# Two-layer cross-attention on one core: 32x32 transpositions on VectorE in layer 0, and its exponential as 16 small ScalarE instructions

## The chip, the cores and the metric

The kernel runs on one core of one Trainium2 chip. The metric is device time in microseconds (us) of that core. The kernel before took 2107.89 us in the median of three runs (2104.96 to 2112.77).

## The reference

Two cross-attention layers follow each other on x, 4 batches of 1024 tokens with 1024 features, with one context of 64 rows for each batch. Everything is float32.

```
layer 0   q = x @ Wq + bq            32 heads of 32 features
          k = ctx @ Wk + bk          8 key heads, each shared by 4 query heads
          v = ctx @ Wv + bv
          attn = softmax(q.k / sqrt(32) + mask)      over 64 keys
          x = layernorm(attn.v @ Wo + bo + x) * gamma + beta
layer 1   a = layernorm(ctx); q = x @ Wq.T; k, v = a @ Wk.T, a @ Wv.T
          16 heads of 64, softmax over 64 keys
          x = x + tanh(gate) * (attn.v @ Wo.T)
```

## The kernel before, in words

Every product is made exact enough by splitting both operands in a high and a low part: the high part is a cast to the matmul's float32 format, the low part is what is left. The helper `three` (L53 to L55) then issues three matmuls for one product. Whoever needs a product therefore needs ScalarE for the high part, and VectorE or GpSimd for the low part, of both operands.

The program has three stages: layer 0's attention, layer 0's output (with the preparation of layer 1's matrices in a table of slots), and layer 1. The change lies nearly all in the first stage.

That stage first prepares the context (turned by TensorE, projected to keys and values, split, and stored in scratch memory), and then runs 64 units: 8 blocks of 512 tokens times 8 key heads g, each with its group of 4 query heads. For one unit the steps are:

- the query of 128 features by 512 tokens, 24 matmuls with Wq as weights; ScalarE adds the bias and makes the high part qs (L528), VectorE the low part (L671);
- the scores of 4 x 128 tokens against 4 heads x 64 keys, 12 matmuls with a block-diagonal key tile kb;
- VectorE adds the mask out of PSUM into pr (L677) and takes the maximum of each of 16 (token tile, head) rows (L682); GpSimd subtracts it (L783); ScalarE takes the exponential of all 1024 elements in one instruction (L546); VectorE sums (L694) and inverts (L698); GpSimd multiplies (L786);
- TensorE turns the probabilities, eight transpositions of 128x128 (L411), into PSUM; ScalarE makes the high part pTh (L541), VectorE the low part pTl (L689);
- six matmuls with the block-diagonal value tile vb; ScalarE copies the result to ot (L533), and SP stores it in o_scratch.

The tiles of x are turned by TensorE as well, eight transpositions (L328) for each tile of 128 tokens; `next_x(u)` says in which units: every second one, for the block that follows. ScalarE and VectorE split them (L490, L610).

The order is written out by hand for each engine in a loop over u, and a wait on a semaphore stands ahead of each instruction that needs one. In its iteration u an engine works on the query of unit u, the scores of unit u-1 and the probabilities of unit u-2, and so on: the units overlap. An engine takes its instructions strictly in this order. SP loads kb and vb for each unit out of scratch memory, four DMAs each, and issues them in its own order. Mask and x tiles are double-buffered, pr is held three times, the turned probabilities once.

Of the kernel before, what the change touches and what calls it, by code (L numbers as in the profile page):

```python
# [16 lines left out]
F32 = mybir.dt.float32  # L17
# [6 lines left out]
P = 128  # L24
# [51 lines left out]
def layer0(nc, ps, ident, d, w):  # L76
    with ExitStack() as mem:
# [13 lines left out]
        xr = [at(f"xr{i}", 144 + 4 * i, [P, D]) for i in range(2)]  # L91
# [9 lines left out]
        vst = [at(f"vst{r}", 140 + 2 * r, [P, 2, KV0], F32R) for r in range(2)]  # L101
        kf, vf = at("kf", 196, [P, 2, CTX]), at("vf", 198, [P, 2, KV0])

        qs = [[at(f"qs{i}{x}", 152 + 4 * i + 2 * j, [P, BLK], F32R) for j, x in enumerate("hl")] for i in range(2)]
        kb = [at(f"kb{i}", 160 + 2 * i, [P, 2, GRP, KEYS], F32R) for i in range(2)]
        vb = [at(f"vb{i}", 164 + 2 * i, [P, 2, 2, P], F32R) for i in range(2)]
        pr = [at(f"pr{i}", 168 + 4 * i, [P, TPB, GRP, KEYS]) for i in range(3)]
        pT = [at(f"pT{x}", 180 + 4 * j, [P, 2, BLK], F32R) for j, x in enumerate("hl")]
        ot = [at(f"ot{i}", 188 + 2 * i, [P, BLK]) for i in range(2)]
# [25 lines left out]
        bq, bk, bv_row = part(0, KT), part(8, 2), at("bv", 200, [P, KV0])  # L135
# [8 lines left out]
        S, TR = ps[:, 1024:2048], ps[:, 2048:3072]  # L144
        V = [ps[:, 3072 + HALF * i:][:, :HALF] for i in range(2)]
        C2 = ps[:, 0:2048]
        O, TT = Q, S
# [11 lines left out]
        wq_ld, x_ld, k_ld, v_ld, o_st = sems("wq_ld", KT), sems("x_ld", 2), sems("k_ld", 2), sems("v_ld", 2), sems("o_st", 2)  # L159
# [16 lines left out]
        def sync_attention(sp):  # L176
            sp.dma_start(ctx[:], d["ctx"].rearrange("(r p) d -> p r d", p=P)).then_inc(ctx_ld, 16)
            for n in range(2):
                sp.dma_start(xr[n][:], d["x"][P * n:P * (n + 1), :]).then_inc(x_ld[n], 16)
# [7 lines left out]
            for k in range(3):  # L187
                sp.dma_start(wqr[:, k], w["Wq0"][P * k:P * (k + 1), :]).then_inc(wq_ld[k], 16)
            for n in range(2, 4):
                sp.wait_ge(x_turned, n - 1)  # L190
                sp.dma_start(xr[n % 2][:], d["x"][P * n:P * (n + 1), :]).then_inc(x_ld[n % 2], 16)
            for k in range(3, KT):
                sp.dma_start(wqr[:, k], w["Wq0"][P * k:P * (k + 1), :]).then_inc(wq_ld[k], 16)
            sp.dma_start(mask[0][:], d["mask"][0:BLK, :].rearrange("(m p) s -> p m s", p=P)).then_inc(mask_ld, 16)
            for h in range(2):
                sp.wait_ge(k_hi, h + 1)
                sp.wait_ge(k_lo, h + 1)
                sp.dma_start(d["k"][h], f32(kst[h][:]).rearrange("p b x s -> p b (x s)")).then_inc(kv_st, 16)
            for r in range(2):
                sp.wait_ge(v_hi, r + 1)  # L200
                sp.wait_ge(v_lo, r + 1)
                sp.dma_start(d["v"][r], f32(vst[r][:])).then_inc(kv_st, 16)
            sp.wait_ge(kv_st, 64)
            sp.wait_ge(zeroed, 4)

            def load_k(u):
                t, g = divmod(u, KT)
                h, a = divmod(g, 4)
                src = d["k"][h, HD0 * a:HD0 * (a + 1), t // 2, :].rearrange("p (x s) -> p x s", x=2)
                for j in range(GRP):  # L210
                    sp.dma_start(f32(kb[u % 2][HD0 * j:HD0 * (j + 1), :, j, :]), src).then_inc(k_ld[u % 2], 16)

            def load_v(u):
                t, g = divmod(u, KT)
                r, a = divmod(t // 2, 2)
                src = d["v"][r, KEYS * a:KEYS * (a + 1), :, HD0 * g:HD0 * (g + 1)]
                for i in range(2):
                    for c in range(2):
                        o = HD0 * (2 * c + i)
                        sp.dma_start(f32(vb[u % 2][KEYS * i:KEYS * (i + 1), :, c, o:o + HD0]), src).then_inc(v_ld[u % 2], 16)  # L220

            load_k(0)
            load_v(0)
            for u in range(UNITS + 3):
                t, g = divmod(u, KT)
                if u < UNITS and u % 2 == 0 and (n := 4 + u // 2) < NTILE:
                    after(sp, x_turned, n - 1)
                    sp.dma_start(xr[n % 2][:], d["x"][P * n:P * (n + 1), :]).then_inc(x_ld[n % 2], 16)
                if u + 1 < UNITS:
                    after(sp, scores, u)  # L230
                    load_k(u + 1)
                if g == 2 and t + 1 < NBLK:
                    after(sp, s_read, 8 * t)
                    sp.dma_start(mask[(t + 1) % 2][:], d["mask"][BLK * (t + 1):BLK * (t + 2), :]
                                 .rearrange("(m p) s -> p m s", p=P)).then_inc(mask_ld, 16)
                if 2 <= u <= UNITS:
                    after(sp, pv, u - 2)
                    load_v(u - 1)
                if u >= 3:
                    v = u - 3  # L240
# [8 lines left out]
        def sync_output(sp):  # L249
            def load_chunk(c):  # L250
                t, a = divmod(c, BLK // CHUNK)
                for i in range(2):
                    sp.wait_ge(o_st[i], 16 * 4 * (t + 1))
                after(sp, o_done, 4 * (c - 1))
                sp.dma_start(oc[c % 2][:], d["o"][t, :, :, CHUNK * a:CHUNK * (a + 1)].rearrange("g p c -> p g c"))\
                    .then_inc(oc_ld[c % 2], 16)
# [68 lines left out]
        def tensor_attention(pe):  # L325
            def turn(out, src, done):
                for k in range(KT):
                    last = nc.tensor.transpose(out[:, P * k:P * (k + 1)], src[:, P * k:P * (k + 1)], ident[:])  # L328
                last.then_inc(done, 1)

# [6 lines left out]
            def turn_x(n):  # L337
                pe.wait_ge(x_ld[n % 2], 16 * (n // 2 + 1))
# [885 lines left out]
```

## Time and profile before

| | |
|---|---|
| median of 3 runs | 2107.89 us |
| the profiled execution | 2110.65 us, its span 2108.9 us |
| mean granted TensorE clock | 0.976 |
| TensorE busy (matmul) | 1960.3 us, 93% |
| VectorE busy | 1003.8 us, 48% |
| GpSimd busy | 763.4 us, 36% |
| ScalarE busy | 580.7 us, 28% |

The shares are means over three stages with different limits, so they say little on one of them. The views in the section on rows are taken from the stage that is changed. In a timeline a row is one instruction or several alike: its start, its duration, engine, line, operation, output and inputs, and in brackets the engine's idle time before it with what ended it. In a table of windows a row gives a stretch, its length, the busy time of PE, PEld, DVE, ACT and POOL with the number of instructions, PEclk, the DMA engines' share and GB/s. Matmuls overlap, so their pace is the distance from start to start, and not the duration. PEclk is the clock that TensorE was granted, where 1.00 is 2.4 GHz and 0.50 is 1.2 GHz.

### The profile page before, as it was taken

How to read it: one execution, taken by the hardware profiler on the slowest of the kernel's cores; microseconds unless marked ns; L12 is line 12 of the kernel's file. 1: busy time of each engine (PE TensorE's matmuls, PEld its weight loads, DVE VectorE, ACT ScalarE, POOL GpSimd, SP SyncE). 2: the span in 40 equal slices, each digit the busy share in tenths (PEclk: the TensorE clock that was granted, in tenths of full speed). 3: DMA queues.
4: the chain of work that ended last, by engine and by line, in shares of the span. 5: the costliest groups of instructions: out<-in, count | busy, mean ns of one | idle time of the engine just before them, and what ended most of it. 6: DMA issues, size and time to landing. Idle time of an engine off the chain costs nothing. (4 is left out here: it accounts for less than half of the span.)

```text
span 2108.9 us, 24271 instructions
## 1 busy us (share of the span) xinstructions
PE 1960.3 (93%) x9664; PEld 1613.5 (77%) x9664; DVE 1003.8 (48%) x1061; ACT 580.7 (28%) x674; POOL 763.4 (36%) x480
## 2 busy tenths in 40 slices
PE   6999999999999869999999995899999999999998
PEld 5777777777777657788888874688778878877887
DVE  6555555555555544444444433623453264345322
ACT  4333333333333333222323221311221131122110
POOL 1333333333333344546455453511341152134111
PEclk8999999999999979999999997999999999999999
DMA  6212212222223146565546643331331133113100
GB/s 238 59 55 60 69 58 69 60 68 61 68 60 118 40 164 202 197 219 180 198 167 211 203 160 137 136 116 41 119 121 50 50 121 120 40 40 130 50 30 30
DMA packets 181694, 227.77 MB, mean 108 GB/s; under 512 B 70480, under 2 KB 130000, under 8 KB 181584
## 3 DMA queue, kind: packets, MB, share of 16 engines
q1 hardware_dynamic: 181584, 226.20, 31.6%
q8 instruction: 81, 1.33, 0.3%
q14 instruction: 29, 0.24, 0.0%
HBM read 141.20 MB, written 84.93 MB: 107 GB/s over the span
## 5 line engine op out<-in xcount | busy, mean ns | idle before, releaser
L1159 POOL TENSOR_TENSOR prob<-prob,mx 128x1024 f32<-128x1024 f32 x32 | 61.0, 1907 | 452.2 <-DVE mx L1126 452.2
L53 PE MATMUL ps<-Ah,x2Tl 128*128 128x512 f32 x512 | 205.2, 401 | 8.2 <-POOL Al L939 7.2
L783 POOL TENSOR_TENSOR pr<-pr,small 128x1024 f32<-128x1024 f32 x64 | 121.9, 1905 | 246.1 <-DVE small L682 246.1
L53 PE MATMUL ps<-Bh,probTl 128*128 128x512 f32 x512 | 202.3, 395 | 2.4 <-DVE probTl L1141 2.4
L55 PE MATMUL ps<-Ah,x2Th 128*128 128x512 f32 x512 | 201.9, 394 | 0.0
L54 PE MATMUL ps<-Al,x2Th 128*128 128x512 f32 x512 | 201.8, 394 | 0.0
L55 PE MATMUL ps<-Bh,probTh 128*128 128x512 f32 x512 | 199.7, 390 | 0.0
L54 PE MATMUL ps<-Bl,probTh 128*128 128x512 f32 x512 | 199.2, 389 | 0.0
L786 POOL TENSOR_TENSOR pr<-pr,small 128x1024 f32<-128x1024 f32 x64 | 122.1, 1907 | 212.6 <-DVE small L698 212.6
L1122 DVE SCALAR_TENSOR_TENSOR prob<-ps,bias 128x1024 f32<-128x1024 f32 x32 | 39.1, 1223 | 238.0 <-PE ps L55 238.0
L677 DVE TENSOR_TENSOR pr<-ps,mask 128x1024 f32<-128x1024 f32 x64 | 78.4, 1224 | 147.9 <-PE ps L55 147.9
L541 ACT CAST pTh<-ps 128x1024 fp32r<-128x1024 f32 x64 | 65.2, 1018 | 271.6 <-PE ps L411 271.6
L798 POOL TENSOR_TENSOR xb<-xb,bo 128x1024 f32<-128x1024 f32 x32 | 78.6, 2458 | 157.6 <-DMA xb<-in_x_dram 149.3
L689 DVE TENSOR_TENSOR pTl<-ps,pTh 128x1024 fp32r<-128x1024 f32 x64 | 78.4, 1225 | 117.9 <-ACT pTh L541 117.9
L738 DVE TENSOR_TENSOR y<-ps,xb 128x512 f32<-128x512 f32 x64 | 44.2, 690 | 178.2 <-PE ps L55 171.2
L53 PEld LDWEIGHTS ps<-Ah,x2Tl 128*128 128x128 f32 x512 | 98.3, 192 | 28.4 <-issue 9.0
L53 PE MATMUL ps<-wo0h,oc0l 128*128 128x512 f32 x256 | 102.7, 401 | 15.8 <-POOL oc0l L793 15.8
L55 PEld LDWEIGHTS ps<-Ah,x2Th 128*128 128x128 f32 x512 | 97.6, 191 | 20.8
L1057 ACT CAST x2Th<-ps 128x1024 fp32r<-128x1024 f32 x32 | 32.5, 1015 | 292.4 <-PE ps L1001 292.4
L54 PEld LDWEIGHTS ps<-Al,x2Th 128*128 128x128 f32 x512 | 98.0, 191 | 19.5
L53 PEld LDWEIGHTS ps<-Bh,probTl 128*128 128x128 f32 x512 | 96.2, 188 | 21.4 <-DVE probTl L1141 2.6
L55 PEld LDWEIGHTS ps<-Bh,probTh 128*128 128x128 f32 x512 | 96.1, 188 | 20.4
(186 smaller groups left out, 4900.3 us busy)
## 6 DMA issues: line engine op xcount, KB each, us to landing
xr<-in_x_dram SPq DMA_DIRECT2D x32, 512.0 KB, 3.7
o_scratch<-ot SPq DMA_DIRECT2D x64, 256.0 KB, 2.3
xb<-in_x_dram SPq DMA_DIRECT2D x32, 512.0 KB, 5.1
ocr<-o_scratch SPq DMA_DIRECT2D x16, 1024.0 KB, 6.5
a_scratch<-ost SPq DMA_DIRECT2D x64, 256.0 KB, 3.0
x_scratch<-y SPq DMA_DIRECT2D x32, 512.0 KB, 3.3
b_scratch<-ost SPq DMA_DIRECT2D x64, 256.0 KB, 2.3
x2t<-x_scratch SPq DMA_DIRECT2D x32, 512.0 KB, 3.3
```

The lines of the kernel that those rows point to most:

```text
L53: nc.tensor.matmul(out, a[1], b[0], start=start, stop=False)
L54: nc.tensor.matmul(out, a[0], b[1], start=False, stop=False)
L55: return nc.tensor.matmul(out, a[0], b[0], start=False, stop=stop)
L541: nc.scalar.copy(pT[0][:].rearrange("p c n -> p (c n)"), TR).then_inc(p_hi, 1)
L677: nc.vector.tensor_tensor(p[:], S.rearrange("p (m j s) -> p m j s", m=TPB, j=GRP), mask[t % 2][:].unsqueeze(2).to_broadcast([P, TPB, GRP, ...
L689: nc.vector.tensor_tensor(pT[1][:].rearrange("p c n -> p (c n)"), TR, f32(pT[0][:]).rearrange("p c n -> p (c n)"), ALU.subtract).then_inc( ...
L738: nc.vector.tensor_tensor(y[n % 3][:, cols], O[half], xb[n % 2][:, cols], ALU.add).then_inc(y_done, 1)
L783: nc.gpsimd.tensor_tensor(heads, heads, mx.unsqueeze(2).to_broadcast([P, TPB * GRP, KEYS]), ALU.subtract)\
L786: nc.gpsimd.tensor_tensor(heads, heads, rs.unsqueeze(2).to_broadcast([P, TPB * GRP, KEYS]), ALU.mult)\
L798: nc.gpsimd.tensor_tensor(xb[n % 2][:], xb[n % 2][:], bo0[:], ALU.add).then_inc(xbo, 1)
L1122: nc.vector.scalar_tensor_tensor(out=pr[:], in0=S.rearrange("p (h s) -> p h s", h=H1), scalar=SCALE1, in1=bias[:, bass.ds(b, 1), :].to_bro ...
L1159: nc.gpsimd.tensor_tensor(pr[:], pr[:], mx[:].unsqueeze(2).to_broadcast([P, H1, KEYS]), ALU.subtract).then_inc(centered, 1)
```

## The change

TensorE no longer turns x or the probabilities. VectorE's transposition turns 32x32 blocks only, so the rest of the way is taken by other orders of the data:

- x, Wq, the mask, the context and the stored output are loaded and stored with other access patterns. An x tile now comes in as four DMAs of 32 partitions each, and VectorE turns it in one instruction into xTr (`turn_x`). Wq's rows, keys and values are permuted to match, and keys and values are stored together in one scratch tensor in 12 DMAs.
- The token order inside a block is (token // 4, token % 4), so the query is read out of PSUM with a step of 4, and ot is written with a step of 4. The loads of o_scratch in the output stage are eight DMAs of 32 partitions in place of one.
- The probabilities are turned by one VectorE transposition of 128x1024 elements (L695 of the changed kernel) into pTr, in SBUF. ScalarE copies the high part from there, and the low part goes from VectorE to GpSimd.
- VectorE takes the maximum negated. GpSimd no longer subtracts it, and VectorE no longer sums: ScalarE takes the exponential in 16 instructions of 64 elements with the negated maximum as bias, and each writes its sum to sm.
- The scores have two PSUM regions, since the one for the turned data is free. pr is held twice in place of three times, the turned probabilities twice in place of once.
- The values of a unit are now multiplied three iterations behind the query in place of two, and the loop is one iteration longer.
- In the output stage GpSimd no longer waits for the last stores of ot ahead of its clearing of bd.

The core of the diff:

```
@@ tensor_attention, loop over u
-                    after(pe, s_read, v)
+                    after(pe, s_read, v - 1)
 ...
-                n = next_x(u) if u < UNITS else None
-                if n is not None:
-                    after(pe, p_lo, u - 2)
-                    turn_x(n)
 ...
-                    pe.wait_ge(probs, v + 1)
 ...
-                    for c in range(2):
-                        for m in range(TPB):
-                            last = nc.tensor.transpose(TR[:, BLK * c + P * m:][:, :P], pr[v % 3][:, m, 2 * c:2 * c + 2, :]
-                                                       .rearrange("p j s -> p (j s)"), ident[:])
-                    last.then_inc(p_turned, 1)
 ...
-                if u >= 2:
-                    v = u - 2
+                if u >= 3:
+                    v = u - 3
                     pe.wait_ge(p_lo, v + 1)

@@ scalar_attention
+            for u in range(UNITS + 4):
+                if u >= 4:
+                    v = u - 4
                     act.wait_ge(pv, v + 1)
                     after(act, o_st[v % 2], 16 * (v // 2))
+                    nc.scalar.copy(ot[v % 2][:].rearrange("p (j i m) -> p j m i", j=GRP, m=TPB),
+                                   V[v % 2].rearrange("p (j m i) -> p j m i", j=GRP, m=TPB)).then_inc(o_ev, 1)
+                if 2 <= u < UNITS + 2:
+                    v = u - 2
+                    act.wait_ge(maxed, v + 1)
+                    after(act, recips, v)
+                    heads = pr[v % 2][:].rearrange("p j m s -> p (j m) s")
+                    for e in range(TPB * GRP):
+                        last = nc.scalar.activation(heads[:, e], heads[:, e], ACT.Exp, bias=mx[:, e:e + 1],
+                                                    accum_out=sm[:, e:e + 1])
+                    last.then_inc(exped, 1)
+                if u < UNITS:
+                    if (n := next_x(u)) is not None:
+                        split_x(n)
+                    act.wait_ge(q_done, u + 1)
+                    after(act, scores, u - 1)
+                    nc.scalar.activation(qs[u % 2][0][:], Q[u % 2].rearrange("p (n m) -> p m n", m=TPB), ACT.Identity,
+                                         bias=bq[:, u % KT:u % KT + 1]).then_inc(q_hi, 1)
                 if 2 <= u < UNITS + 2:
                     v = u - 2
                     act.wait_ge(p_turned, v + 1)
+                    nc.scalar.copy(pT[v % 2][0][:], pTr[v % 2][:]).then_inc(p_hi, 1)

@@ vector_attention
+            for u in range(UNITS + 2):
+                if 1 <= u <= UNITS and (n := next_x(u - 1)) is not None:
+                    split_x(n)
+                if u >= 2:
+                    v = u - 2
+                    dve.wait_ge(exped, v + 1)
+                    after(dve, probs, v)
+                    nc.vector.reciprocal(rs, sm).then_inc(recips, 1)
+                if u < UNITS and (n := next_x(u)) is not None:
+                    turn_x(n)
+                if 1 <= u <= UNITS:
 ... mask addition, then
+                    nc.vector.tensor_reduce(mx, p[:].rearrange("p j m s -> p (j m) s"), AX_X, ALU.max, negate=True).then_inc(maxed, 1)
                 if u >= 2:
                     v = u - 2
+                    dve.wait_ge(probs, v + 1)
+                    after(dve, pv, v - 1)
+                    nc.vector.transpose(pTr[v % 2][:].rearrange("p b j n -> p b (j n)").rearrange("p b (h i) -> p h b i", i=32),
+                                        pr[v % 2][:].rearrange("p j m (b i) -> p (j m) b i", b=2)).then_inc(p_turned, 1)
+                if u < UNITS:
+                    dve.wait_ge(q_hi, u + 1)
 ... the low part of the query

@@ pool_attention
+            for u in range(2, UNITS + 3):
+                if u >= 3:
+                    v = u - 3
+                    pool.wait_ge(p_hi, v + 1)
+                    nc.gpsimd.tensor_tensor(pT[v % 2][1][:], pTr[v % 2][:], f32(pT[v % 2][0][:]), ALU.subtract).then_inc(p_lo, 1)
+                if 2 <= u < UNITS + 2:
+                    v = u - 2
+                    pool.wait_ge(recips, v + 1)
+                    nc.gpsimd.tensor_tensor(heads(v), heads(v), rs.unsqueeze(2).to_broadcast([P, TPB * GRP, KEYS]), ALU.mult)\
+                        .then_inc(probs, 1)

@@ sync_output, load_chunk
+                for i in range(2):
+                    for j in range(GRP):
+                        sp.dma_start(oc[c % 2][32 * j:32 * (j + 1), :, P * i:P * (i + 1)],
+                                     d["o"][t, :, 32 * (2 * a + i):32 * (2 * a + i + 1), P * j:P * (j + 1)]
+                                     .rearrange("g p c -> p g c")).then_inc(oc_ld[c % 2], 16)
```

The order of instructions shows what the loops come to. ScalarE before, in an iteration that splits a tile of x, in the middle of the stage (the semaphores that an instruction waits for stand in brackets; a_centered comes from GpSimd, a_p_turned and a_pv from TensorE):

```order
L528 ACTIVATE qs0h<-ps,small 128x512 [waits a_scores,a_q_done]
L533 COPY ot_90<-ps 128x512 [waits a_o_st0,a_pv]
L490 CAST xT1h<-ps 128x8x128 [waits a_x_turned]
L541 CAST pTh<-ps 128x1024 [waits a_pv,a_p_turned]
L546 ACTIVATE pr_85<-pr_85 128x1024 [waits a_centered]
```

ScalarE in the changed kernel, one iteration of the same kind (a_maxed, a_p_turned and a_x_turned come from VectorE now):

```order
L514 COPY ot_96<-ps 128x4x4x32 [waits a_o_st1,a_pv]
L522 ACTIVATE pr_88,small<-pr_88,small 128x64 [waits a_recips,a_maxed]
L522 ACTIVATE pr_88,small<-pr_88,small 128x64 x15
L476 CAST xT1h<-xT1r 128x8x128 [waits a_x_turned]
L530 ACTIVATE qs1h<-ps,small 128x512 [waits a_scores,a_q_done]
L535 CAST pT1h<-pT1r 128x1024 [waits a_p_turned]
```

The exponentials now stand directly behind the copy to ot, ahead of the high parts of x, of the query and of the probabilities. The cast to pT, which waits for VectorE, stands last.

VectorE before, one iteration with the split of an x tile:

```order
L671 SCALAR_TENSOR_TENSOR qs0l<-ps,small,qs0h 128x512 [waits a_q_hi]
L677 TENSOR_TENSOR pr_85<-ps,mask_92 128x1024 [waits a_scores,a_p_turned]
L682 TENSOR_REDUCE small<-pr_85 128x16 [waits a_centered,a_s_read]
L610 TENSOR_TENSOR xT1l<-ps,xT1h 128x8x128 [waits a_x_hi]
L689 TENSOR_TENSOR pTl<-ps,pTh 128x1024 [waits a_p_hi]
L694 TENSOR_REDUCE small<-pr_85 128x16 [waits a_exped]
L698 RECIPROCAL small<-small 128x16 [waits a_probs,a_summed]
```

VectorE in the changed kernel, an iteration that turns an x tile (L600):

```order
L674 RECIPROCAL small<-small 128x16 [waits a_probs,a_exped]
L600 STREAM_TRANSPOSE xT1r<-xr_59 128x4x8x32 [waits a_q_done,a_x_ld1]
L684 TENSOR_TENSOR pr_87<-ps,mask_97 128x4x4x64 [waits a_scores]
L690 TENSOR_REDUCE small<-pr_87 128x16 [waits a_exped,a_s_read]
L695 STREAM_TRANSPOSE pT1r<-pr_88 128x16x2x32 [waits a_pv,a_probs]
L699 SCALAR_TENSOR_TENSOR qs1l<-ps,small,qs1h 128x512 [waits a_q_hi]
```

The reciprocal has moved ahead of the mask addition (L684) and waits for ScalarE there (a_exped); the low part of the query stands last.

## Rows read from the trace of the kernel before

**Rows 1.** Table of windows, the stretch of layer 0's attention.

```profile
57.10:725.50 668.40, 622.82 (x3356) 511.77 (x3355) 388.01 (x406) 231.43 (x278) 240.19 (x126) 1.00 0.23 66
```

**Rows 2.** Query for line L677: count, durations, first and last start.

```profile
L677 DVE TENSOR_TENSOR pr<-ps,mask x64: 1223/1225/1226, 57.1 to 725.5; 128x1024 f32<-128x1024 f32 x64
```

**Rows 3.** Timeline of TensorE in one step: start, duration, what, idle time before.

```profile
399.99 0.40 PE L54 MATMUL ps<-xT0l,wq0h 128*128 128x512 f32 x1
400.23 0.40 PE L55 MATMUL ps<-xT0h,wq0h 128*128 128x512 f32 x1
...
402.94 1.06 PE L411 MATMUL ps<-ident,pr 128*128 128x128 f32 x8 [0.93 <-DVE xT1l L610]
...
409.35 0.28 PE L54 MATMUL ps<-kb,qs1h 128*128 128x256 f32 x1
409.46 0.28 PE L55 MATMUL ps<-kb,qs1h 128*128 128x256 f32 x1
```

**Rows 4.** Timeline of VectorE, the same step.

```profile
399.18 1.23 DVE L677 TENSOR_TENSOR pr<-ps,mask 128x1024 f32<-128x1024 f32 x1 [2.12 <-PE ps L55]
400.44 1.22 DVE L682 TENSOR_REDUCE small<-pr 128x16 f32<-128x1024 f32 x1
401.58 1.22 DVE L610 TENSOR_TENSOR xT1l<-ps,xT1h 128x1024 fp32r<-128x1024 f32 x1
...
407.48 0.25 DVE L698 RECIPROCAL small<-small 128x16 f32<-128x16 f32 x1
407.65 0.66 DVE L671 SCALAR_TENSOR_TENSOR qs1l<-ps,small,qs1h 128x512 fp32r<-128x512 f32 x1
410.94 1.23 DVE L677 TENSOR_TENSOR pr<-ps,mask 128x1024 f32<-128x1024 f32 x1 [2.63 <-PE ps L55]
```

**Rows 5.** Timeline of ScalarE, the same step.

```profile
404.05 1.02 ACT L541 CAST pTh<-ps 128x1024 fp32r<-128x1024 f32 x1 [3.07 <-PE ps L411]
404.95 1.06 ACT L546 ACTIVATE pr<-pr 128x1024 f32<-128x1024 f32 x1
```

**Rows 6.** Groups of ScalarE by shape: count, busy us, mean ns, idle before.

```profile
L546 ACT ACTIVATE pr<-pr 128x1024 f32<-128x1024 f32 x64 | 67.9, 1060 | 26.4 <-POOL pr L783 26.4
...
L533 ACT COPY ot<-ps 128x512 f32<-128x512 f32 x64 | 37.7, 589 | 65.1 <-PE ps L55 65.0
...
L528 ACT ACTIVATE qs1h<-ps,small 128x512 fp32r<-128x512 f32 x32 | 22.0, 687 | 2.8
...
L553 ACT CAST oc0h<-ocr 128x1024 fp32r<-128x1024 f32 x16 | 16.0, 1049 | 8.8 <-DMA ocr<-o_scratch 8.7
...
L1060 ACT ACTIVATE gt<-gate 128x1 f32<-128x1 f32 x1 | 0.2, 202 | 12.9 <-DMA gate<-in_L_xattn_gate_dram 12.9
```

**Rows 7.** Timeline of GpSimd, the same step.

```profile
407.81 1.91 POOL L786 TENSOR_TENSOR pr<-pr,small 128x1024 f32<-128x1024 f32 x1 [4.16 <-DVE small L698]
```

**Rows 8.** Groups of GpSimd by shape.

```profile
L786 POOL TENSOR_TENSOR pr<-pr,small 128x1024 f32<-128x1024 f32 x64 | 122.1, 1907 | 212.6 <-DVE small L698 212.6
...
L793 POOL TENSOR_TENSOR oc0l<-ocr,oc0h 128x1024 fp32r<-128x1024 f32 x16 | 39.0, 2458 | 21.4 <-ACT oc0h L553 21.4
```

**Rows 9.** Table of windows in layer 1, around an idle TensorE.

```profile
1508.00:1512.00 4.00, 3.05 (x12) 2.77 (x13) 3.29 (x3) 0.98 (x1) 4.00 (x2) 0.58 0.00 0
1512.00:1516.00 4.00, 4.00 (x19) 3.28 (x18) 1.22 (x1) 0.04 (x1) 2.58 (x2) 1.00 0.57 184
```

**Rows 10.** Timeline of TensorE there, at the idle time.

```profile
1508.95 1.97 PE L1045 MATMUL ps<-ident,prob 128*128 128x128 f32 x8 [2.31 <-POOL prob L1165]
```

**Rows 11.** Timeline of ScalarE, the last copy to ot.

```profile
741.91 0.59 ACT L533 COPY ot<-ps 128x512 f32<-128x512 f32 x1 [4.28 <-PE ps L55]
```

**Rows 12.** Query for line L255, the loads of chunks.

```profile
L255 SPq DMA_DIRECT2D ocr<-o_scratch x16: 377/381/527, 743.9 to 1245.9; - x16
...
  ACT oc1h L553: 10.0, 4
  ACT oc0h L553: 8.7, 4
```

More of the change, by code:

```diff
@@ L186, in sync_attention @@
             sp.dma_start(bet1[:], row(w["beta1"], D)).then_inc(gb_ld, 16)
-            for k in range(3):
-                sp.dma_start(wqr[:, k], w["Wq0"][P * k:P * (k + 1), :]).then_inc(wq_ld[k], 16)
+            load_wq(0)
             for n in range(2, 4):
                 sp.wait_ge(x_turned, n - 1)
[L191 to L194, printed above, removed]
+                load_x(n)
+            for k in range(2, KT, 2):
+                load_wq(k)
+            load_mask(0)
             for h in range(2):
@@ L197, in sync_attention @@
                 sp.wait_ge(k_lo, h + 1)
-                sp.dma_start(d["k"][h], f32(kst[h][:]).rearrange("p b x s -> p b (x s)")).then_inc(kv_st, 16)
+                for a in range(4):
+                    sp.dma_start(d["kv"][h, :, :, a, :P].rearrange("b p c -> p b c"),
+                                 f32(kst[h][32 * a:32 * (a + 1)]).rearrange("p b x s -> p b (x s)")).then_inc(kv_st, 16)
             for r in range(2):
@@ L201, in sync_attention @@
                 sp.wait_ge(v_lo, r + 1)
-                sp.dma_start(d["v"][r], f32(vst[r][:])).then_inc(kv_st, 16)
-            sp.wait_ge(kv_st, 64)
+                for h in range(2):
+                    sp.dma_start(d["kv"][h, :, :, :, P + 64 * r:P + 64 * (r + 1)].rearrange("b p g c -> (b p) g c"),
+                                 f32(vst[r][:, 4 * h:4 * (h + 1)]).rearrange("p g x d -> p g (x d)")).then_inc(kv_st, 16)
+            sp.wait_ge(kv_st, 16 * 12)
             sp.wait_ge(zeroed, 4)
@@ L227, in sync_attention @@
                     after(sp, x_turned, n - 1)
-                    sp.dma_start(xr[n % 2][:], d["x"][P * n:P * (n + 1), :]).then_inc(x_ld[n % 2], 16)
-                if u + 1 < UNITS:
-                    after(sp, scores, u)
+                    load_x(n)
+                if 1 <= u and u + 1 < UNITS:
+                    sp.wait_ge(scores, u)
                     load_k(u + 1)
+                if 3 <= u <= UNITS:
+                    sp.wait_ge(pv, u - 2)
+                    load_v(u - 1)
                 if g == 2 and t + 1 < NBLK:
                     after(sp, s_read, 8 * t)
[L234 to L240, printed above, removed]
+                    load_mask(t + 1)
+                if u >= 4:
+                    v = u - 4
                     sp.wait_ge(o_ev, v + 1)
@@ L325, in tensor_attention @@
         def tensor_attention(pe):
[L326 to L329, printed above, removed]
             def turn_ctx():
@@ L385, in tensor_attention @@
                 if u < UNITS:
-                    query(range(0, 2))
+                    query(range(0, 4))
                 if 1 <= u <= UNITS:
@@ L421, in tensor_attention @@
                     for c in range(2):
-                        last = three(nc, V[v % 2], [vb[v % 2][:, x, c] for x in (0, 1)], [pT[x][:, c] for x in (0, 1)],
+                        last = three(nc, V[v % 2], [vb[v % 2][:, c, x] for x in (0, 1)], [pT[v % 2][x][:, c].rearrange("p j n -> p (j n)") for x in (0, 1)],
                                      c == 0, c == 1)
@@ L563, in diagonal @@
                     r = slice(HD1 * h, HD1 * (h + 1))
[L564 removed]
+                    last = nc.scalar.copy(bd[i][0][r, :, h, :].rearrange("p b (r i) -> p b r i", r=2), PJ[i][r].rearrange("p (r b i) -> p b r i", r=2, b=BATCH))
                 last.then_inc(bd_hi, 1)
@@ L815, in pool_output @@
             pool.wait_ge(pv, UNITS)
-            for i in range(2):
-                pool.wait_ge(o_st[i], 16 * UNITS // 2)
             for i in range(2):
```

211 lines of the change are left out of this document (86 added, 125 removed).

## The prediction

> **What bounds the kernel now.** I read the stretch of layer 0's attention first, since nearly all edits lie in its 64 steps. The table of windows shows TensorE busy 622.82 of 668.40 us there, at a granted clock of 1.00, beside 388.01 us on VectorE, 231.43 us on ScalarE and 240.19 us on GpSimd [rows 1]. The query for the mask addition L677 gives the step: 64 of them from 57.1 to 725.5 us, so 668.4 / 63 = 10.61 us each [rows 2]. The timelines by engine then show one step at close range. TensorE runs one matmul of 512 columns each 0.24 us or a little less and one of 256 columns each 0.12 us, and spends 1.06 us on the eight turns of probabilities, with 0.93 us of idle time ahead of them [rows 3]. VectorE waits 2.12 and 2.63 us for TensorE before L677 [rows 4], and ScalarE 3.07 us for the turned probabilities [rows 5]. So TensorE sets the step, and the others have room.
>
> **The change on TensorE.** Per step it loses eight turns of probabilities, and in 28 of the 63 steps eight turns of x. What stays is 30 matmuls of 512 columns (24 for the query, 6 for the values) and 12 of 256: 30 x 0.23 + 12 x 0.12 = 8.3 us [rows 3]. If TensorE still set the step, 63 x (10.61 - 8.3) = 146 us would go. Whether it does depends on the loop that the new order builds between ScalarE and VectorE.
>
> **The new loop.** On VectorE the reciprocal of head group u-2 now stands ahead of the mask addition of u-1 and waits for the sixteenth exponential of u-2. The transposition of u-2 stands behind mask addition and maximum of u-1. On ScalarE the copy of the turned probabilities of u-2 waits for that transposition, and the exponentials of u-1 stand behind this copy and behind the copy to ot. So the chain is closed: exponentials of u-2, reciprocal, mask addition of u-1, maximum of u-1, transposition of u-2, copy to pTh, copy to ot, exponentials of u-1. Before, none of it was serial in this way: the exponential of u-1 shared no chain with the reciprocal of the group before. Its terms, from start to start:
> - copy to ot: 0.589 us [rows 6] less the 0.1 us by which ScalarE instructions in a row overlap (404.05 + 1.02 against the next start at 404.95, [rows 5]): 0.49. It is now written with a step of four elements, which no row shows; nothing to a second 0.59, and I take nothing.
> - reciprocal: 407.48 to 407.65, 0.17, and 0.1 for a semaphore (it ends at 407.73 and GpSimd starts at 407.81, [rows 4, 7]): 0.27.
> - mask addition: 399.18 to 400.44 [rows 4]: 1.26. Same elements, other order of writing; I take the same.
> - maximum, now negated: 400.44 to 401.58 [rows 4]: 1.14.
> - transposition of 1024 elements in 32x32 blocks: no row shows one. Every VectorE pass over 1024 f32 elements in rows 4 takes 1.21 to 1.23 us; I take 1.2 and a semaphore of 0.05: 1.25. Bounds: 0.6 (two elements at a time) to 2.4 (two passes).
> - copy to pTh, now out of SBUF: 1.049 us as for oc0h [rows 6], less 0.1: 0.95.
> Together 0.49 + 0.27 + 1.26 + 1.14 + 1.25 + 0.95 = 5.36 us beside the exponentials. The GpSimd product of 1.907 us [rows 8] runs beside mask addition and maximum (2.4 us) and costs nothing; without that cover it would add 1.9. The removed centring, the removed sum and the lo part that goes from VectorE to GpSimd (1.2 us off VectorE, 2.458 us as for oc0l onto GpSimd, [rows 8]) are not in the loop: GpSimd then holds 1.9 + 2.5 = 4.4 us per step. In the 28 steps that turn x, the transposition of x stands between reciprocal and mask addition: 28/63 x 1.15 = 0.51 us on the mean. The loop is 5.87 us plus E, the time of sixteen exponentials.
>
> **E.** One exponential of 1024 takes 1060 ns and a one-element activation 202 ns [rows 6], so (1060 - 202) / 1023 = 0.84 ns per element, and 64 elements take 255 ns. The bias from memory adds 687 - 589 = 98 ns (qs1h against ot, both 128x512, [rows 6]): about 350 ns for one alone, 0.24 us from start to start at the usual overlap of 0.11. What the sum taken along costs no row shows. Lower bound nothing: 0.24 each, E = 3.8. Upper bound a separate instruction of 202 ns with no overlap at all: 0.55 each, E = 8.8. With the read overlapped it is 0.24 + 0.09 = 0.33, with a read that waits for its exponential's end 0.35 + 0.20 - 0.11 = 0.44. I take 0.36, nearer to the overlapped form because the rows in rows 5 overlap: E = 5.8, against one exponential of 1.06 us before. Loop: 5.87 + 5.8 = 11.65 us.
>
> By the Trainium skill, ScalarE: Activation LUTs, section What ACT_TABLE_LOAD costs, an activation with a bias from memory takes 280 ns + 0.833 ns per element and overlaps its neighbour by about 93 ns, which is 240 ns for 64 elements; the trace's rows agree with that. It has no price for the accumulator output, so by it alone E is an estimated 3.84 us. The skill's VectorE: DVE Perf Modes, section on the TRN2 errata, speaks against the change: each small tile pays the fixed latency again, and it wants 512 elements or more. The rows here carry the same point: 16 x 0.24 = 3.8 us against 1.06 us.
>
> **Steps and edges.** 63 x (11.65 - 10.61) = +66 us. TensorE then idles about 3.3 us a step, in one piece ahead of the scores, where it waits for qs lo, which stands last in VectorE's iteration. Such a gap has a price in this trace: after 2.31 us of idle time the granted clock was 0.58 over the 4 us in which TensorE resumed [rows 9, 10]. Here that costs some 1.5 us of TensorE per step, and lies inside the gap: 8.3 + 1.5 is under 11.65, so I count 0. Start: VectorE transposes four x tiles more, 4 x 1.15 = 4.6, and two units more of stores and loads stand ahead of the loop: +6. End: one stage more of pipeline behind the last mask addition, where before it took 741.91 + 0.59 - 725.5 = 17.0 us [rows 2, 11]: the maximum, E, reciprocal, product, transposition, copy, lo part, values, copy to ot make about 21: +4. Output stage: each of 16 chunk loads is eight DMAs in place of one at 0.38 us of issue, 2.7 us later, with smaller packets, and ScalarE waited for these loads eight times [rows 12]; 0 to 8 x 2.7 = 22, I take +3, as TensorE hides most waits there. SP gets three more x DMAs in every second step (4 x 0.38 us by the same row), which lie in its waits. Sum: 66 + 6 + 4 + 3 = +79 on the profiled run's own 2110.65 us (its span of 2108.9 and 1.75 around it), 2190 us; that run lies 2.8 us above the median of 2107.89, so I say 2186 (2189.4 less 2.8). The edges are 13 us of it.
>
> **Rivals.**
> - The sum costs nothing (pitch 0.24). The loop is 9.7 us, 63 x -0.9 + 13 = -44: 2064 us. For it: the overlap seen between ScalarE instructions, and that TensorE's floor of 8.3 leaves room. Against it: an output of its own to write sixteen times. The deciding point is E = 10.4 - 5.87 = 4.5 us, a pitch of 0.28. Faster than before below it.
> - The sum is read serially, 0.44 to 0.55 each: E 7.0 to 8.8, loop 12.9 to 14.7, and with the 13 us of the edges +157 to +271: 2265 to 2379 us. A transposition at two passes gives the same size at my pitch: (1.15 + 0.51) x 63 = +105 on the forecast, 2291 us. For it: the added bounds all lie above. Against: no such gap in the rows.
> - TensorE's clock stays at its lower level of 1.2 GHz because of the gaps: its 8.3 us become 16.6, it sets the step, and 63 x 6.0 + 13 gives 2499 us. Against it: the clock was back at 1.00 in the 4 us after the fall [rows 9].
> - Nothing measurable (the pitch happens on 0.28): 2108.
>
> **Numbers.** Forecast 0.57, its own range 2130 to 2265 (pitch 0.30 to 0.44); sum free 0.19; serial read or slow transposition 0.18; clock 0.02; no change 0.04. Half a per cent is about what a measurement of this kernel tells from no change. Faster 0.19, same 0.04, slower 0.77. The range 2085 to 2300 leaves out about 0.12 of the free case and 0.08 of the dear ones.
>
> **What would show it.** In the new profile: 64 mask additions about 11.6 us apart; VectorE's reciprocal waiting for ScalarE's exponentials; ScalarE waiting some 4 us for the transposition each step; TensorE waiting for qs lo ahead of the scores and busy about 75% of the stretch. The start-to-start time of the small exponentials decides: at 0.24 the kernel is faster, at 0.36 or more it is slower. A mask addition that waits for TensorE again, or ScalarE idle while VectorE waits for scores, would make the loop wrong.

## The result and the profile after

The changed kernel takes 2203.96 us (median of 4 runs, 2200.70 to 2204.68), the kernel before 2108.78 us (4 runs, 2104.96 to 2112.77). The ratio is 1.0448, 95% interval 1.0426 to 1.0471: 4.5% slower. The forecast was 2186 us, range 2085 to 2300. The profiled span is 2202.3 us at a mean granted clock of 0.943, 93.4 us longer than before.

The attention of layer 0 first. The query for the mask addition, now L684, and the table of windows over its stretch answer to [rows 1, 2]:

```profile
L684 DVE TENSOR_TENSOR pr<-ps,mask x64: 1160/1184/1225, 65.6 to 795.5; 128x1024 f32<-128x1024 f32 x64
```

```profile
65.60:795.50 729.90, 575.03 (x2628) 472.58 (x2626) 335.48 (x370) 519.10 (x2229) 279.52 (x124) 0.91 0.20 60
```

729.9 / 63 = 11.59 us a step where it was 10.61. TensorE's share fell from 93% to 79% of the stretch, and ScalarE's busy time more than doubled, from 231.43 to 519.10 us. The timeline of VectorE shows one turn of the loop (columns as in [rows 4]):

```profile
401.31 0.25 DVE L674 RECIPROCAL small<-small 128x16 f32<-128x16 f32 x1 [5.54 <-ACT pr L522]
401.48 1.16 DVE L684 TENSOR_TENSOR pr<-ps,mask 128x1024 f32<-128x1024 f32 x1
402.67 1.22 DVE L690 TENSOR_REDUCE small<-pr 128x16 f32<-128x1024 f32 x1
403.81 1.24 DVE L695 STREAM_TRANSPOSE pT0r<-pr 128x1024 f32<-128x1024 f32 x1
404.97 0.71 DVE L699 SCALAR_TENSOR_TENSOR qs0l<-ps,small,qs0h 128x512 fp32r<-128x512 f32 x1
412.33 0.25 DVE L674 RECIPROCAL small<-small 128x16 f32<-128x16 f32 x1 [6.66 <-ACT pr L522]
412.50 1.19 DVE L600 STREAM_TRANSPOSE xT0r<-xr 128x1024 f32<-128x1024 f32 x1
```

And that of ScalarE in the same step:

```profile
405.08 1.05 ACT L535 CAST pT0h<-pT0r 128x1024 fp32r<-128x1024 f32 x1 [3.23 <-DVE pT0r L695]
406.03 1.08 ACT L514 COPY ot<-ps 128x512 f32<-128x512 f32 x1
406.90 0.33 ACT L522 ACTIVATE pr<-pr,small 128x64 f32<-128x64 f32 x1
407.13 0.19 ACT L522 ACTIVATION_READ_ACCUMULATOR pr<-pr,small 128x1 f32 x1
407.23 0.33 ACT L522 ACTIVATE pr<-pr,small 128x64 f32<-128x64 f32 x1
...
412.12 0.19 ACT L522 ACTIVATION_READ_ACCUMULATOR pr<-pr,small 128x1 f32 x1
413.72 1.04 ACT L476 CAST xT0h<-xT0r 128x1024 fp32r<-128x1024 f32 x1 [1.42 <-DVE xT0r L600]
```

Each of the two engines stands while the other works: VectorE 5.54 and 6.66 us for the sixteenth exponential, ScalarE 3.23 us for the turned probabilities. The mask addition waits for nothing in this step (7.6 us in 8 of the 64), where before it waited 2.12 and 2.63 us for TensorE [rows 4]. TensorE now waits for VectorE, here 0.99 us for the low part of the query (PE timeline), and over the stretch 101 us for this and 52.5 us for the last turned x tile at seven block starts:

```profile
405.73 0.39 PE L53 MATMUL ps<-kb,qs0l 128*128 128x256 f32 x1 [0.99 <-DVE qs0l L699]
```

The groups of ScalarE by shape in this stretch, which answer to [rows 6]:

```profile
L522 ACT ACTIVATE pr<-pr,small 128x64 f32<-128x64 f32 x1008 | 334.6, 337 | 0.0
L522 ACT ACTIVATION_READ_ACCUMULATOR pr<-pr,small 128x1 f32 x1008 | 193.0, 191 | 0.0
L514 ACT COPY ot<-ps 128x512 f32<-128x512 f32 x61 | 66.5, 1090 | 0.0
```

Each exponential with a sum is two instructions, 337 and 191 ns, and a pair starts 0.33 us after the last one (406.90, 407.23).

By stages, the 93.4 us of the span are the differences between first and last starts in the two traces:

| stretch | before | after | measured | predicted |
|---|---|---|---|---|
| start to the first mask addition | 57.1 | 65.6 | +8.5 | +6 |
| 63 steps | 668.4 | 729.9 | +61.5 | +66 |
| last mask addition to the first y | 44.7 | 51.5 | +6.8 | +4 |
| first to last y (output stage) | 521.6 | 536.2 | +14.6 | +3 |
| last y to the end | 817.1 | 819.1 | +2.0 | 0 |

The output stage is the one far off. Its loads and who waited for them (us in all, times), from the query for L274, which answers to [rows 12]:

```profile
L274 SPq DMA_DIRECT2D ocr<-o_scratch x128: 303/451/1857, 818.8 to 1338.3; - x128
...
  ACT oc0h L542: 16.1, 5
  ACT oc1h L542: 11.9, 4
```

Theory after this reading: the loop between ScalarE and VectorE sets the step; the change holds a gain (the turns taken off TensorE) and a loss (the sixteen exponentials), tied by the order of the loop; and the output stage loses by the eight loads of each chunk. Rival: the loss lies in the transpositions or in TensorE's lower clock, and the exponentials are incidental.

### The profile page after: what moved, and what is told of

It is laid out like the page before. It is cut to its first block and busy times, and to the rows that moved or that the text cites. A ratio compares the mean times of both kernels' runs of the same rounds, so it can differ in the third digit from the quotient of the medians.

```text
span 2202.3 us, 24852 instructions
## 1 busy us (share of the span) xinstructions
PE 1911.2 (87%) x8896; PEld 1572.3 (71%) x8896; DVE 958.1 (44%) x1029; ACT 874.9 (40%) x2658; POOL 806.0 (37%) x480
## 3 DMA queue, kind: packets, MB, share of 16 engines
q1 hardware_dynamic: 205184, 226.21, 31.9%
q8 instruction: 74, 1.21, 0.2%
## 5 line engine op out<-in xcount | busy, mean ns | idle before, releaser
L522 ACT ACTIVATE pr<-pr,small 128x64 f32<-128x64 f32 x1024 | 339.9, 337 | 0.0
L793 POOL TENSOR_TENSOR pr<-pr,small 128x1024 f32<-128x1024 f32 x64 | 122.0, 1906 | 280.9 <-DVE small L674 280.9
L522 ACT ACTIVATION_READ_ACCUMULATOR pr<-pr,small 128x1 f32 x1024 | 196.0, 191 | 0.0
L674 DVE RECIPROCAL small<-small 128x16 f32<-128x16 f32 x64 | 16.2, 253 | 392.6 <-ACT pr L522 392.6
L805 POOL TENSOR_TENSOR xb<-xb,bo 128x1024 f32<-128x1024 f32 x32 | 77.4, 2419 | 183.3 <-DMA xb<-in_x_dram 174.9
L53 PE MATMUL ps<-xT0h,wq0l 128*128 128x512 f32 x256 | 107.3, 419 | 37.8 <-DVE xT0l L607 37.8
L53 PE MATMUL ps<-xT1h,wq0l 128*128 128x512 f32 x256 | 107.6, 420 | 30.0 <-DVE xT1l L607 30.0
L789 POOL TENSOR_TENSOR pT1l<-pT1r,pT1h 128x1024 fp32r<-128x1024 f32 x32 | 89.2, 2788 | 115.4 <-ACT pT1h L535 115.4
L1086 ACT CAST probTh<-ps 128x1024 fp32r<-128x1024 f32 x32 | 32.5, 1016 | 211.8 <-PE ps L1050 211.8
```

The costliest lines, as they stand in the source:

```text
L53: nc.tensor.matmul(out, a[1], b[0], start=start, stop=False)
L522: last = nc.scalar.activation(heads[:, e], heads[:, e], ACT.Exp, bias=mx[:, e:e + 1], accum_out=sm[:, e:e + 1])
L789: nc.gpsimd.tensor_tensor(pT[v % 2][1][:], pTr[v % 2][:], f32(pT[v % 2][0][:]), ALU.subtract).then_inc(p_lo, 1)
L793: nc.gpsimd.tensor_tensor(heads(v), heads(v), rs.unsqueeze(2).to_broadcast([P, TPB * GRP, KEYS]), ALU.mult)\
L805: nc.gpsimd.tensor_tensor(xb[n % 2][:], xb[n % 2][:], bo0[:], ALU.add).then_inc(xbo, 1)
```

## Experiments

All ratios are to the kernel before on the same chip, where its median was 2108.2 to 2109.4 us. "Step" is the mean distance of two mask additions. A block is eight steps, those of one group of 512 tokens. The edits are shortened to what they change, some of them in words.

| kernel | us | ratio, 95% | step, us |
|---|---|---|---|
| before | 2108.78 | 1 | 10.61 |
| changed | 2203.96 | 1.0426 to 1.0471 | 11.59 |
| no_sum | 2118.47 | 1.0027 to 1.0062 | 10.27 |
| turn_only | 2027.55 | 0.9599 to 0.9631 | 8.87 |
| exp_only | 2334.78 | 1.1050 to 1.1088 | 14.18 |
| ot_plain | 2186.99 | 1.0354 to 1.0389 | 11.29 |
| chunk_one | 2184.64 | 1.0337 to 1.0377 | 11.59 |
| late_cast | 2083.28 | 0.9854 to 0.9925 | 9.75 |
| turn_early | 2000.45 | 0.9464 to 0.9511 | 8.43 |
| turn_late_early | 1984.22 | 0.9390 to 0.9437 | 8.19 |
| exps_late_early | 2041.52 | 0.9662 to 0.9705 | 9.03 |
| store_four | 1968.28 | 0.9313 to 0.9352 | 8.20 |

**no_sum**: the changed kernel without the sum output; sm is filled once, so the probabilities are not divided by their sum.

```
- nc.scalar.activation(..., ACT.Exp, bias=mx[:, e:e + 1], accum_out=sm[:, e:e + 1])
+ nc.scalar.activation(..., ACT.Exp, bias=mx[:, e:e + 1])
```

> The changed kernel, whose sixteen exponentials don't take the sum along; sm is filled once with 64, so the probabilities come out unnormalised by their true sum. Loop theory (ScalarE and VectorE form one serial chain, and the exponentials' pace is a term of it): the pair of exponential and read takes 0.333 us from start to start, the exponential alone should take 0.24, so the chain loses 16 x 0.093 = 1.5 us a step; steps of 10.1 us, kernel 2204 - 63 x 1.5 = 2110 us. Rival (TensorE with its gaps, or ScalarE's busy time, sets the step): ScalarE's busy time falls too, but a step set by TensorE would not move, 2204 us.

Confirmed in the main: 2118 us where 2110 was expected. ScalarE's timeline:

```profile
400.07 1.10 ACT L514 COPY ot<-ps 128x512 f32<-128x512 f32 x1
400.95 1.29 ACT L522 ACTIVATE pr<-pr,small 128x64 f32<-128x64 f32 x5
```

Sixteen exponentials then take 3.92 us, 0.245 each. The sum output costs 0.09 us each, and 2203.96 - 2118.47 = 85 us in all, nearly the whole loss. Inside a block the step falls by 1.49 us (11.07 to 9.58, and 12.14 to 10.66 with a turn of x), the 1.5 that was expected; the mask addition's waits for TensorE at block starts grow from 7.6 to 18.4 us and take the rest back. This is the forecast's rival "sum free", and it came out near the time of before, not below; the section on the prediction says why.

**turn_only**: the changed kernel with maximum, centring, one exponential and sum as before. **exp_only**: the kernel before with the sixteen exponentials alone:

```
(in words)
- pool: centre pr by mx;  act: exp of 1024;  dve: sum of pr
+ dve: maximum negated;   act: 16 exp of 64 with bias=mx, accum_out=sm
```

> The changed kernel with all its transpositions on VectorE, but the softmax as before: GpSimd subtracts the maximum, one exponential of 1024, VectorE sums. Loop theory: the chain exponential, sum, reciprocal, mask addition, maximum, transposition, cast, copy to ot is 0.96 + 0.05 + 1.14 + 0.17 + 1.19 + 1.14 + 1.27 + 0.95 + 0.87 = 7.7 us, 8.9 in the steps that turn x, below or at TensorE's 8.3 and its waits: steps of 8.4 to 8.9 us, kernel 2204 - 63 x 2.9 = 2020 us, range 2000 to 2040, which is faster than the 2109 of before. Rival (the transpositions themselves cost the time, by VectorE's load or strided operands): 2110 us or more.

> The kernel before with only the softmax edit: sixteen exponentials with the maximum as bias and the sum taken along, TensorE still turns x and the probabilities. Loop theory: VectorE's reciprocal of unit v stands ahead of the low part of the next query there, so the chain is exponentials 5.4, reciprocal 0.3, low part 0.7, scores 1.5, mask addition 1.25, maximum 1.2, 10.3 us and semaphores of 0.3, 10.6, against 10.61 of before, and 1 us more in the steps in which TensorE turns x: steps of 10.6 to 11.2 us, 2110 to 2150 us. Rival (the small exponentials cost by ScalarE's load alone, which has room): 2109 us, no change. Rival (the exponentials are the whole loss, whatever stands around them): 2204 us.

turn_only confirmed its expectation: the transpositions on VectorE alone gain 81 us. exp_only missed it by 185 us: alone, the exponentials cost 226 us, not 1 to 41. The two effects do not add (-81 + 226 is not +95). ScalarE and then VectorE in exp_only:

```profile
407.40 0.33 ACT L548 ACTIVATE pr<-pr,small 128x64 f32<-128x64 f32 x1
407.64 0.19 ACT L548 ACTIVATION_READ_ACCUMULATOR pr<-pr,small 128x1 f32 x1
407.73 0.67 ACT L528 ACTIVATE qs1h<-ps,small 128x512 fp32r<-128x512 f32 x1
408.30 0.57 ACT L533 COPY ot<-ps 128x512 f32<-128x512 f32 x1
415.48 1.01 ACT L541 CAST pTh<-ps 128x1024 fp32r<-128x1024 f32 x1 [6.62 <-PE ps L411]
```

```profile
408.43 0.75 DVE L675 SCALAR_TENSOR_TENSOR qs1l<-ps,small,qs1h 128x512 fp32r<-128x512 f32 x1 [0.32 <-ACT qs1h L528]
411.32 1.22 DVE L681 TENSOR_TENSOR pr<-ps,mask 128x1024 f32<-128x1024 f32 x1 [2.15 <-PE ps L55]
```

In that order the query's high part is queued behind the exponentials (402.41 to 407.83). Its low part, the scores, nine query matmuls and the turns of the probabilities follow in turn, and only then the cast and the next exponentials (at 416.39, so this turn of the loop is 13.98 us). TensorE stands on the loop there:

```profile
409.23 0.39 PE L53 MATMUL ps<-kb,qs1l 128*128 128x256 f32 x1 [2.35 <-DVE qs1l L675]
...
411.44 0.63 PE L54 MATMUL ps<-xT1l,wq0h 128*128 128x512 f32 x1
411.87 0.63 PE L55 MATMUL ps<-xT1h,wq0h 128*128 128x512 f32 x1
...
414.41 0.27 PE L411 MATMUL ps<-ident,pr 128*128 128x128 f32 x1
```

Its matmuls of 512 columns are 0.43 us apart here, against 0.24 in [rows 3]. The table of windows gives the granted clock, 1.00 where TensorE resumes after 2.35 us of idle time and 0.50, the lower of its two levels (1.2 GHz), behind it:

```profile
408.00:410.00 2.00, 0.77 (x6) 0.77 (x7) 0.86 (x2) 0.86 (x2) 1.81 (x1) 1.00 0.00 0
411.00:413.00 2.00, 2.00 (x7) 1.61 (x6) 1.64 (x2) 0.00 (x0) 0.00 (x0) 0.50 0.08 16
```

For the same matmuls TensorE is busy 709.4 us over the steps where it was 622.8 before, so the clock accounts for at most 87 of the 226 us, an upper bound, and the serial order for the larger part. I had left both, the place of the query's part and the clock, out of the expectation. In the changed kernel TensorE is off the loop, and the same sixteen instructions cost less there: 176 us, from turn_only's 2027.55 to 2203.96.

**ot_plain**: ot is copied in the order of PSUM, with no step, so the tokens are in a wrong order in the output.

```
- nc.scalar.copy(ot[...] "p (j i m) -> p j m i", V[...] "p (j m i) -> p j m i")
+ nc.scalar.copy(ot[v % 2][:], V[v % 2])
```

> The changed kernel, whose copy to ot is written in plain order and no longer with a step of four, so the tokens come out in another order. Loop theory: the copy is a term of the chain and falls from 1.09 to 0.59 us as in the kernel before, so 0.4 to 0.5 us a step go: 2204 - 63 x 0.45 = 2176 us. Rival (the copy lies beside the chain): 2204 us.

Partly: the copy falls from 1090 to 580 ns, the step by 0.30 us and the time by 17 us, where 0.45 a step was expected. Inside a block the step falls by 0.38 us (11.07 to 10.68, 12.14 to 11.77), which is what the copy loses from start to start (0.87 to 0.48): it is a full term of the loop. Most of the rest is taken back at block starts, where the mask addition's waits for TensorE grow from 7.6 to 12.0 us. The edit changes only the order in which SBUF is written, PSUM is read in the same order in both, so the writing is what costs. The step of four in it was taken at nothing in the prediction.

**chunk_one**: the changed kernel with one DMA for each chunk instead of eight, in the order of before, so o's tokens and heads reach the wrong places.

> The changed kernel with one DMA for each chunk of o_scratch as before, so the output stage reads its tokens and features in another order. Issue theory (eight issues keep SP from its other transfers and delay the chunk): the output stage gives back most of its 14.6 us and the first chunk comes 4 us sooner, 2204 - 15 = 2189 us, range 2185 to 2195. Rival (the output stage is longer for another reason): 2204 us.

Confirmed, 0.4 us below the range: the attention is unchanged, and first to last y is 519.0 us against 536.2 (521.6 before). The first y comes 1.9 us sooner, not 4. ScalarE's groups again wait about as in [rows 6, 12], 9.5 and 10.0 us, and the time falls by 19.3 us. GpSimd's wait for the loads of xb, which SP issues behind the eight, was 149.3 us before and 174.9 in the changed kernel, and is 154.3 here.

```profile
L539 ACT CAST oc0h<-ocr 128x1024 fp32r<-128x1024 f32 x16 | 16.0, 1048 | 9.5 <-DMA ocr<-o_scratch 9.5
```

**late_cast**: the copy to pTh, the lo part and the values one iteration later, with three turned buffers. The loop then has neither cast nor transposition in it.

```
- if 2 <= u < UNITS + 2:  v = u - 2;  copy(pT[v % 2][0], pTr[v % 2])
+ if 3 <= u < UNITS + 3:  v = u - 3;  copy(pT[v % 3][0], pTr[v % 3])
```

> The changed kernel, sixteen exponentials and all, with one move: ScalarE casts the turned probabilities of a unit one iteration later, behind the next unit's exponentials, and the steps behind it (lo part, values, copy to ot) follow one iteration later; the turned probabilities are held three times. Loop theory: transposition, cast and copy to ot drop out of the chain, which leaves exponentials 5.4, semaphore 0.1, reciprocal 0.17, mask addition 1.19, maximum 1.14 and a semaphore, 8.1 us (9.2 in steps that turn x), beside ScalarE's own 5.3 + 0.95 + 0.87 + 0.58 = 7.7 us and TensorE's 8.3: steps of 8.6 us plus some 0.5 for the waits at the starts of blocks, 2204 - 63 x 2.5 + 4 = 2050 us. Rival (the exponentials' own 4 us more of ScalarE are the loss wherever they stand): 2204 us.

The loop was the bound: 1.84 us a step and 121 us less, by an edit that removes no work, and this version is 1.1% faster than before. The size was over-expected: 2083 us, not 2050. The exponentials now wait for the maximum only 1.5 us in the whole stretch, so the loop through VectorE is open. VectorE still waits for the last exponential in each step (2.66 and 3.70 us), as ScalarE's own queue is the longest now: it is busy 515.6 of 614.0 us and waits 40 us more for turned x tiles. From mask addition to mask addition a step inside a block is 9.06 or 9.19 us, where 8.6 was expected. The mean of 9.75 comes from the block starts, where TensorE waits up to 5.4 us for the low part of the last x tile and the next mask addition for TensorE; they cost about 45 us (this stretch less that of exps_late_early below, which has the same steps inside a block), where 0.5 us a step, 32 us, was expected:

```profile
400.99 0.26 DVE L675 RECIPROCAL small<-small 128x16 f32<-128x16 f32 x1 [3.70 <-ACT pr L523]
...
406.42 2.08 DVE L608 TENSOR_TENSOR xT1l<-xT1r,xT1h 128x1024 fp32r<-128x1024 f32 x1
411.16 0.25 DVE L675 RECIPROCAL small<-small 128x16 f32<-128x16 f32 x1 [2.66 <-ACT pr L523]
...
438.77 1.19 DVE L685 TENSOR_TENSOR pr<-ps,mask 128x1024 f32<-128x1024 f32 x1
452.32 1.22 DVE L685 TENSOR_TENSOR pr<-ps,mask 128x1024 f32<-128x1024 f32 x1 [4.42 <-PE ps L55]
464.18 1.18 DVE L685 TENSOR_TENSOR pr<-ps,mask 128x1024 f32<-128x1024 f32 x1
```

**turn_early**: turn_only with x turned in even in place of odd steps and its loads one tile ahead, so that the last turned tile of a block no longer ends just as TensorE needs it (turn_only waits 3.88 us for xT1l at 409.12). **turn_late_early**: both edits.

```
- return 4 * (t + 1) + g // 2 if g % 2 and t + 1 < NBLK else None
+ return 4 * (t + 1) + g // 2 if g % 2 == 0 and t + 1 < NBLK else None
```

> The version with the transpositions on VectorE and the softmax of before, whose x tiles are turned in the even units of a block in place of the odd ones, with their loads issued one tile ahead, so the last tile is split one unit before the next block begins. Expected: the waits of TensorE for the last x tile at seven block starts (about 4 us each) go, 2028 - 22 = 2006 us, range 1998 to 2015. Rival (the waits at block starts are made up within the block): 2028 us.

> The same as the version that turns x in the even units, and in addition the cast of the turned probabilities one iteration later, as a candidate for the fastest version. Loop theory: the chain between ScalarE, VectorE and GpSimd falls from 7.7 and 8.9 us to about 7.1 and 8.2 and TensorE's 8.3 us sets every step: steps of 8.35 us, one step more of pipeline, 2000 us, range 1992 to 2012. Rival (the chain was covered by TensorE already): as the other version or 3 us more.

turn_early is confirmed. turn_late_early went the way expected, but at 1984 us it lies 16 us below the expected time and 8 us below its range: the step is 8.19 us and not 8.35. The turn gives 0.44 us a step, the cast 0.24. At 8.19 us the step is about the 8.3 us that the prediction gave TensorE's remaining matmuls.

**exps_late_early**: this best order with the sixteen exponentials and sums put back.

> The kernel with transpositions on VectorE, the cast one iteration later and x turned in the even units, and again the sixteen exponentials with their sums in place of one exponential, the centring and the sum. Theory (ScalarE's time is the bound once the cast is off the loop): sixteen exponentials with sums hold ScalarE 5.3 us where one holds it 1.06, so its iteration is exps 5.3 + cast 0.95 + copy to ot 1.0 + query parts and a wait, 9.0 to 9.5 us a step where the version with one exponential has 8.2: 2035 to 2070 us, and the exponentials cost 50 to 85 us by themselves even in the best order found. Rival (the loop through VectorE was their only price, so with it broken they are free): 1984 us, as with one exponential.

Confirmed: 2041.52 us, 57 us above its twin with one exponential. The table of windows over its 569.2 us of steps:

```profile
67.00:636.20 569.20, 530.08 (x2622) 435.33 (x2620) 356.29 (x368) 516.84 (x2228) 262.70 (x123) 1.00 0.26 75
```

ScalarE is busy 91% of them, and its waits fill nearly all of the rest, 38.8 us of them for turned x tiles; its exponentials wait for the maximum only 2.9 us. TensorE is busy 530.08 us at a clock of 1.00. So even off the serial loop the exponentials cost 0.84 us a step, by ScalarE's queue: its own time, and the wait for the x tile, which VectorE turns only behind the reciprocal and so behind the exponentials. How the 0.84 us divide between the two was not tested.

**store_four**: turn_late_early with the permutation moved from the loads of o_scratch to the stores: four stores in each step, one load for each chunk.

```
- for i, j: dma(oc[32j.., :, P i..], d["o"][t, :, 32(2a + i).., P j..])
+ dma(oc[c % 2][:], d["o"][t, a])
- dma(d["o"][t, g], ot)
+ for q in range(4): dma(d["o"][t, q // 2, :, g, P (q % 2)..], ot[32 q..])
```

> The fastest kernel so far (turns on VectorE, one exponential, late cast, x turned early), with the permutation of the stored output moved from the loads to the stores: ot is stored by four DMAs in place of one in each attention step, and each of the 16 chunk loads is one DMA in place of eight. Theory (the eight loads in a row were the loss of the output stage, 19 us there, and SP has 3 us of waits left in an attention step): first to last y falls from 534.5 to about 520 us, the attention's step stays at 8.2 us, 1965 us in all. Rival (three more issues of 0.4 to 0.6 us in each attention step delay the key and value loads on SP): the step grows to 8.5 us or more, 1984 us or above.

Confirmed, and the fastest of all: 1968.28 us, 6.7% below before, 10.7% below the changed kernel. The window over its steps, and the query for its loads:

```profile
66.00:582.60 516.60, 515.04 (x2619) 439.69 (x2618) 418.86 (x431) 244.23 (x275) 407.53 (x186) 1.00 0.32 82
```

```profile
L278 SPq DMA_DIRECT2D ocr<-o_scratch x16: 326/371/398, 603.3 to 1102.9; - x16
...
  ACT oc0h L540: 8.7, 4
  ACT oc1h L540: 7.4, 3
```

TensorE is busy in 515.04 of 516.60 us at a clock of 1.00: it bounds this stage again. First to last y is 517.9 us.

## Why the prediction came out right, step by step

- **TensorE off the bound, 8.3 us of work left.** Right; turn_late_early and store_four run at 8.2 us a step with TensorE full. The shape of its idle time was only half right: not 3.3 us a step in one piece ahead of the scores, but 1.6 us there (101 / 63), and 7.5 us at each of seven block starts for the last x tile.
- **The closed loop sets the step.** Right: 11.59 us against 11.65, with the waits in the places named, and late_cast shows it by breaking it. ScalarE's wait for the transposition is smaller than the 4 us named, 3.2 us in even and 1.9 in odd steps. The forecast's own sum, 5.87 + 5.8, is 11.67. In an even step the terms, from start to start in the two timelines above, are: reciprocal with its semaphore 0.27 (0.27 predicted), mask addition 1.19 (1.26), maximum 1.14 (1.14), transposition 1.27 (1.25), cast 0.95 (0.95), copy to ot 0.87 (0.49), exponentials 5.33 (5.8). Sum 11.02 against 11.16 without the x turn. Even and odd stand for steps without and with a turn of x.
- **E.** The pitch was 0.333 us where 0.36 was taken; the form "read overlapped", 0.24 + 0.09, was exact. Taking a middle value put 0.47 us too much into the step. That the step came out within 0.06 us is luck: this error and the next one cancel.
- **Copy to ot.** Taken at nothing for its step of four, measured 0.38 us a step. ot_plain got back 0.38 inside a block, 0.30 on the mean.
- **x turn.** 0.51 us predicted; an odd step is 12.13 us, 1.11 over the even one, times 28/63 = 0.49. The mask addition's eight waits for TensorE, 7.6 us in all, were not foreseen.
- **TensorE's gaps and their clock cost nothing.** Right in the changed kernel but for part of those 7.6 us: the mean clock is 0.91 in the stretch and TensorE is busy 575.0 us where turn_late_early, with nearly the same matmuls at 1.00, has 514.8, so 0.96 us a step more (1.5 were estimated), but TensorE was off the loop. It is no general result, as exp_only shows.
- **Edges.** Start +8.5 for 6, end +6.8 for 4, both a little low.
- **Output stage.** The term furthest off: +14.6 us for +3, inside the 0 to 22 given. "TensorE hides most waits there" was wrong. Eight issues took 3.8 to 5.6 us, 4.3 on the mean, not 3.0; ScalarE's waits for them grew from 18.7 to 28.0 us and GpSimd's for xb, issued behind them, from 149.3 to 174.9. chunk_one gets back 19.3 us. Its 11.6 us of error are most of the distance from 2186 to 2204; another 2.8 us are the correction for a profiled run above its median, which did not hold, as the changed kernel's profiled run (2204.06) lay at its median.
- **Rival "sum free".** Its pitch was right (0.245 in no_sum), but it gave 2064 us and the run is 2118: the step is 10.27 us in place of the 9.7 worked out. 0.57 x 63 = 36 of the 54 us are the steps: 0.38 of the 0.57 is the ot copy, and the mask addition's waits for TensorE, 18.4 us in 8 steps, more than make up the rest. The other 18 us are about what the forecast's edges were too low (13 us given, 93.4 - 61.5 = 31.9 measured in the changed kernel). So the point at which the change breaks even lies below a pitch of 0.245, not at 0.28.
- **Theory against rival.** That the transpositions were the loss is refuted by turn_only (ratio 0.9615). The clock was not varied by itself; against it as the loss stands that the mask addition waited for TensorE only 7.6 us in the whole stretch.

What stays open: why writing with a step of four takes the copy nearly twice the time, and how much of what the exponentials cost in the best order is ScalarE's own time.

## What to carry to other kernels

Draw the loop across engines before adding up work: an edit that left TensorE 8.2 us of work a step, where the step had been 10.6, made the kernel slower, and moving one copy by one iteration gave back 121 us with no work removed. Judge the halves of a change apart: here one half was worth -81 us alone and the other +57, +176 or +226 us, depending on the order of the instructions around it. Look at steps inside a block and at its start apart: part of the gains of no_sum and ot_plain was lost at block starts. Count small instructions by their start-to-start distance, and give an access pattern with a step its own price.

## What the runs showed of the hardware

- An exponential of 128x64 with a sum output shows as two ScalarE instructions, 337 and 191 ns, one pair every 0.333 us; without the sum one every 0.245 us.
- ScalarE's copy of 128x512 from PSUM to SBUF takes 589 ns plain and 1090 ns when it writes with a step of four elements (580 in ot_plain, which differs in nothing else). Reading PSUM with a step of four cost nothing measurable: the query's high part, 128x512, takes 678 to 682 ns so in the changed kernel, and 673 to 687 read plainly before.
- VectorE's transposition of 128x1024 f32 in 32x32 blocks takes 1.19 us from a plain input and 1.24 us here, the same as any other pass over 1024 elements [rows 4].
- Eight DMAs of 128 KB in a row were issued in 3.8 to 5.6 us, one of 1 MB in 0.38 [rows 12]. Spread over steps in which their queue was waiting anyway, three more issues a step cost nothing measurable (8.19 and 8.20 us a step).
- The low part of an x tile, a VectorE operation with two SBUF inputs, took 2.02 to 2.07 us on the mean in late_cast (2.08 at 406.42), 1.36 in turn_late_early and 1.21 in the changed kernel. What it ran beside was not varied.
- TensorE was granted a clock of 1.00 as it resumed after 2.35 us of idle time in exp_only, and 0.50 from 411 to 413 us. Over the steps that made 709.4 us of busy time out of 622.8.
